# Row loads with the depth outermost, a limit on how far the maxima run ahead, and the first chunk's tail behind the last maximum

## The reference

```python
q, k, v = x @ Wq.T + bq, x @ Wk.T + bk, x @ Wv.T + bv          # 16 heads of depth 8
scores = einsum('bqhd,bkhd->bhqk', q, k) * attn_scale           # chunk-causal mask (64)
out = softmax(where(mask, -inf, scores)) @ v
x1 = layernorm(x + out @ Wo.T + bo)
sfc = sigmoid(x1 @ gate.T) + bias                               # 4 of 8 groups, then 6 of 32 experts
combine = weights of the chosen six, normalised, * 2.5
y = sum_e combine[:, e] * (silu(x1 @ g_e.T) * (x1 @ u_e.T)) @ d_e.T + shared(x1)
result = layernorm(x1 + y)
```

## Time and profile before

| | us |
|---|---|
| median of 3 runs | 496.4 (492.8 to 497.02) |
| the profiled execution | 494.91 |
| its span | 493.1 |

### The profile page before, as it was taken

One profiled execution on the slowest core, in us unless ns is written; L12 is line 12 of the kernel. 1 busy time (PEld: TensorE's weight loads), 2 busy tenths in 40 slices (PEclk: granted clock), 3 DMA queues, 4 the chain that ended last, 5 costly groups with the idle time before them and its releaser, 6 DMA issues.

```text
span 493.1 us, 7763 instructions
## 1 busy us (share of the span) xinstructions
PE 444.3 (90%) x2665; PEld 210.1 (43%) x2665; DVE 350.3 (71%) x848; ACT 223.1 (45%) x300; POOL 141.9 (29%) x244
## 2 busy tenths in 40 slices
PE   5429999999999999999799879899999999999992
PEld 2302232323333232433223323367676676666660
DVE  2619988888988888777987331286768869965863
ACT  4520016766857767677215369723242243223220
POOL 4061333756746362533213442400000000000000
PEclk9955558999999999998858869999999999999997
DMA  3434214420010101000000030033323322543330
GB/s 117 163 137 148 89 42 141 128 72 26 27 52 24 45 20 50 3 1 1 7 2 2 1 87 1 1 97 103 107 72 100 111 90 86 148 133 105 109 106 21
DMA packets 27031, 34.22 MB, mean 69 GB/s; under 512 B 5745, under 2 KB 16113, under 8 KB 26993
## 3 DMA queue, kind: packets, MB, share of 16 engines
q1 hardware_dynamic: 25862, 33.00, 21.7%
q10 hardware_dynamic: 1130, 0.74, 0.5%
HBM read 29.07 MB, written 4.46 MB: 68 GB/s over the span
## 4 chain that ended last, share of the span: by engine, by line
PE 73%; DVE 13%; DMA 4%; issue 3%; ACTq 3%; ACT 2%; POOL 2%; DVEq 0%; SPq 0%; POOLq 0%
PE ps L1338 13%; PE ps L1255 13%; PE ps L1380 11%; DVE mx L983 9%; PE ps L1353 6%; PE ps L1355 6%; PE ps L1354 6%; PE ps L1321 6%; PE ps L1251 6%; DMA rows_k<-scratch 2%; ACT probs L880 2%; ACTq L568 2%; PE ps L1268 1%; DMA wq<-in_wqT 1%; ACTq L603 1%
## 5 line engine op out<-in xcount | busy, mean ns | idle before, releaser
L983 DVE TENSOR_REDUCE mx<-ps 128x2 f32<-128x256 f32 (+3 forms) x384 | 191.0, 552 | 43.8 <-PE ps L1255 42.4
L880 ACT ACTIVATE probs<-ps 128x1024 f32<-128x1024 f32 (+2 forms) x160 | 142.8, 939 | 76.8 <-PE ps L1321 69.9
L1255 PE MATMUL ps<-rows_k,rows_q 48*128 48x128 bf16 (+3 forms) x576 | 117.6, 313 | 5.2 <-DVE mx L983 3.2
L1338 PE MATMUL ps<-probs,Vg 128*32 128x512 f32 (+3 forms) x768 | 86.8, 526 | 1.2 <-POOL probs L754 1.0
L923 ACT ACTIVATE rows_q<-ps 128x512 f32<-128x512 f32 x68 | 40.7, 599 | 97.3 <-PE ps L1355 94.7
L1255 PEld LDWEIGHTS ps<-rows_k,rows_q 48*128 48x128 bf16 x576 | 35.5, 97 | 91.6 <-DVE mx L983 65.9
L750 POOL TENSOR_SCALAR_AFFINE_SELECT probs<-probs 64x512 f32<-64x512 f32 x64 | 42.4, 662 | 110.4 <-ACT probs L880 108.9
L1353 PE MATMUL ps<-x1hi,w_hi 128*128 128x512 f32 x136 | 74.0, 544 | 0.0
L1321 PE MATMUL ps<-rows_q,rows_k 51*128 51x512 bf16 (+3 forms) x384 | 67.8, 347 | 4.0 <-ACT probs L880 3.9
L1380 PE MATMUL ps<-rows_k,w_down 128*128 128x512 f32 x136 | 69.5, 593 | 0.7 <-DVE rows_k L1199 0.7
L1194 DVE TENSOR_TENSOR rows_q<-ps,rows_q 128x512 f32<-128x512 f32 x64 | 44.1, 689 | 36.2 <-PE ps L1380 34.9
(11 more groups left out here) (105 smaller groups left out, 326.6 us busy)
## 6 DMA issues: line engine op xcount, KB each, us to landing
comb_rows<-weights SPq DMA_DIRECT2D x128, 128.0 KB, 3.0
scratch<-oT SPq DMA_DIRECT2D x8, 384.0 KB, 5.6
w_raw<-in_unitT SPq DMA_DIRECT2D x17, 128.0 KB, 5.7
rows_q<-scratch SPq DMA_DIRECT2D x16, 96.0 KB
rows_k<-scratch SPq DMA_DIRECT2D x14, 96.0 KB
w_down<-in_unitT SPq DMA_DIRECT2D x1, 1088.0 KB, 6.3
xT<-in_xT SPq DMA_DIRECT2D x4, 256.0 KB, 5.6
rows_q<-scratch SPq DMA_DIRECT2D x16, 64.0 KB
```

Source lines behind the costliest of these rows:

```text
L880: act.activation(dst, src, ACT.Exp).then_inc(exps_ready, 1)
L983: dve.tensor_reduce(to, src, AX.X, ALU.max).then_inc(max_read, 1)
L1255: mm = pe.matmul(dst[:, at * m:(at + 1) * m], rows_q[f:f + ROWS, s, p + qt * P:p + (qt + 1) * P], rows_k[f:f + ROWS, s, p + k0:p + k0 + m] ...
L1338: mm = pe.matmul(ps[STRIP * j:STRIP * (j + 1), VALUES * BANK:VALUES * BANK + m], Vg[:, g % 2, kt, j, :], probs[:, (NB * g + b) % SLOTS, j, ...
```

## The change

Four edits. The source of each row load has its depth dimension (8) outermost instead of its part dimension (3 or 2), so the rows land in another order, the same for q and k. The tail of chunk 0 starts behind the last maximum. The planner holds a maximum unit back while it is more than 1.6 groups ahead of the exponentials. The wait for the mask constants stands once ahead of the attention order instead of at the first unit.

```diff
@@ -132,7 +132,7 @@
 
 
 TOP_AFTER = 3
-TAIL_FROM = (NG - 2, 6)
+TAIL_FROM = (NG, 0)
 TOPS_BEFORE = [[t for t in TOPS if t[0] < g_] for g_ in range(NG)]
 MSEQ = max_steps()
 MAX_AT = {step: r for r, step in enumerate(step for step in MSEQ if step[0] in ON_BANK)}
@@ -163,6 +163,7 @@
     ev, vv = ([(g, n) for g in range(NG) for n in range(k)] for k in (NE, NB))
     hop, rows_latency, load = 240, 6000, 6000
     exp_slack, mask_slack = 300, 600
+    lead = 1.6
     t = 0.0
     clock = {"act": 0.0, "pool": 5000.0}
     dve = 0.0
@@ -238,6 +239,8 @@
     def ready_m():
         k = i["m"]
         kind, g, n = MSEQ[k]
+        if kind == "unit" and g + n / NM - i["e"] / NE > lead and i["e"] < len(ev):
+            return far
         out = 0
         if kind in ON_BANK and MAX_AT[kind, g, n] >= RING:
             out = read.get(RSEQ[MAX_AT[kind, g, n] - RING], far)
@@ -587,19 +590,20 @@
         def load_q(eng, g):
             b, r = g // GPB, slice((g % GPB) * STRIP, (g % GPB + 1) * STRIP)
             s = g % NS
-            part = scr[0, b, :, r, :].rearrange("h (d f p) t -> f h d (p t)", d=D, f=2)
+            part = scr[0, b, :, r, :].rearrange("h (d f p) t -> f d h (p t)", d=D, f=2)
+
             for f in range(2):
-                for at, n, src in ((0, 24, part[f]), (24, 16, part[f, 0:2]), (40, 8, part[f, 0])):
+                for at, n, src in ((0, 24, part[f]), (24, 16, part[f, :, 0:2]), (40, 8, part[f, :, 0])):
                     eng.dma_start(rows_q[ROW_HALF * f + at:ROW_HALF * f + at + n, s, :],
                                   src).then_inc(rows_loaded[s], 16)
 
         def load_k(eng, g):
             b, r = g // GPB, slice((g % GPB) * STRIP, (g % GPB + 1) * STRIP)
             s = g % NS
-            part = scr[1, b, :, r, :].rearrange("h (d f p) t -> f h d (p t)", d=D, f=2)
+            part = scr[1, b, :, r, :].rearrange("h (d f p) t -> f d h (p t)", d=D, f=2)
             for f in range(2):
-                for at, n, src in ((0, 24, part[f, 0:1].to_broadcast([3, D, PAIRS * T])),
-                                   (24, 16, part[f, 1:2].to_broadcast([2, D, PAIRS * T])), (40, 8, part[f, 2])):
+                for at, n, src in ((0, 24, part[f, :, 0:1].to_broadcast([D, 3, PAIRS * T])),
+                                   (24, 16, part[f, :, 1:2].to_broadcast([D, 2, PAIRS * T])), (40, 8, part[f, :, 2])):
                     eng.dma_start(rows_k[ROW_HALF * f + at:ROW_HALF * f + at + n, s, :],
                                   src).then_inc(rows_loaded[s], 16)
 
@@ -1224,6 +1228,8 @@
                     mm = pe.matmul(bank(VPROJ[n], P, t * P), xT[:, tt * P:(tt + 1) * P], wv[:, :], start=True, stop=True)
                 mm.then_inc(v_projected, 1)
 
+            pe.wait_ge(masks_loaded, 32)
+
             def max_step(kind, g, n):
 
                 r = MAX_AT[kind, g, n]
@@ -1242,8 +1248,6 @@
                 if kind != "unit":
                     tail_step(kind, g, n)
                     return
-                if r == 0:
-                    pe.wait_ge(masks_loaded, 32)
                 js, qt, k0, m, part = MAXU[g][n]
                 s, dst = g % NS, step_bank((kind, g, n), len(js) * m)
                 if part == 0:

```

## The result

The changed kernel takes 482.5 us (median of 4 runs, 481.63 to 483.17) against 496.6 us for the kernel before on the same chip (492.8 to 497.02). The ratio is 0.973, 95% interval 0.968 to 0.978. The forecast was 480 us, with a range of 472 to 489.

What follows compares the result with a forecast made beforehand. PE was taken to bound the steady part, with DVE near. Gains of 8.0 and 18.2 less costs of 3.3 and 7.5 made -15.4 on 494.91, so 479.5; the median forecast was 480 us, range 472 to 489.

Steps and rivals of the forecast that it cites:

- Term A: Row loads at the start: spread over more DMA engines, the first maximum comes near 26, a gain of 8.0 us.
- The full 8.0 passes: From first maximum to first exponentials and beyond: POOL's splits are off the path, so the whole 8.0 us gain carries on.
- Term B: Weave of chunk 0's tail, from 203 to the last transpose of maxima: 52.0 us instead of 70.2, a gain of 18.2.
- the density estimate of 53.4: Weave without the tail: 53.4 us if DVE keeps the density that it has in the steady part.
- the 54 that the prediction named as a sign of being wrong: Weave up to the last transpose of maxima: a stretch longer than 54 us would show the forecast wrong.
- Term C: From the last transpose of maxima to the first `up`: added chunk 0 and 1 steps cost 3.3 us.
- Term D: Start of the expert loop: first `down` about 11.4 us behind first `up` instead of 5.6, a cost of 7.5 us.
- behind it the hidden product of `i` = 0, for which up(2)'s second half waits: Expert loop start: DVE runs this 0.7 us product behind chunk 1's first route step, holding up(2) and so first `down`.
- U: Time of the first `up`; chunk 1's first route step on DVE was forecast to end 10.0 us behind it.
- That the loads don't spread: Rival for the row loads: they don't spread, or POOL's splits hold the exponentials; gain 0 to 3, 485 to 488; chance 0.10.
- That chunk 1's chain turns all it lacks into PE waits: Rival behind the maxima: chunk 1's chain lacks 9 us, all becoming PE waits; 489 us; chance 0.14.
- That the clock stays at half: Rival from last maximum to the loop's steady part: waits multiply, clock stays at half, +20 us, 500; chance 0.04.

Runs made afterwards that it cites:

- the three kernels with 12, 24 and 34 rows on the fullest one: Changed kernel (12, 482.5 us); changed kernel with the part dimension outermost again in its 16-partition row loads (24, 487.1 us); kernel before (34, 496.6 us).
- loads-only kernel: The kernel before with only the row-load edit of the change, all engine orders as before: 488.4 us, ratio 0.987.
- the kernel with the shared K load: Changed kernel with group 0's six K-load DMAs shared, four issued by ACT and the last two by SP: 480.3 us, ratio 0.967.
- The four kernels of the table above: Changed kernel (482.5 us); with chunk 1's route steps one loop step later (483.7); with the banked-step wait moved ahead of first `down` (484.9); with both (480.3).
- the version with the tail in the last group: Changed kernel with chunk 0's tail woven between the maxima of group 7 instead of behind the last maximum: 480.0 us, ratio 0.970.
- tail alone: Changed kernel with the row loads of before, all else as changed: 488.5 us, ratio 0.987.
- route step later: Changed kernel with chunk 1's route steps one step of the expert loop later: 483.7 us, ratio 0.968.
- banked wait later: Changed kernel with PE's wait for the last three banked steps' readers moved from ahead of up(2) to ahead of first `down`: 484.9 us, ratio 0.979.

## Why the prediction was right, point by point

**Term A, the row loads: the cause was right, the size was not.** That the loads fill more engines with the depth outermost is shown by the packet counts and by the three kernels with 12, 24 and 34 rows on the fullest one. POOL's waits for `w_raw` fell from 19.8 us in two places to 7.8 us in three, and the long queue is gone, though not wholly: the worst landing is 6.4 us, the best still 2.0. Term A took that best landing for the last K row. It was the step that failed: a small transfer's landing stood for that of six loads under way together, and no row showed the two to be alike. The rows land 4.0 us behind the issue (3.4 to 4.0 in seven executions), and the first maximum is at 27.64, not 26. The loads-only kernel (27.06) says the same.

**"The full 8.0 passes" failed as well.** The six stores of the first tops and the splits were not in the way, as argued (first exponential 72.31 before, 65.82 after: 6.5 us earlier, all that the first maximum had gained). Behind it 1.6 us went to a clock that stayed at half for longer, which the prediction had not looked at in that place. It need not have happened: the loads-only kernel has the same loads and a clock of 0.79 there, and loses nothing. In the kernel with the shared K load the clock rose early, and there the tops of group 3 come 8.5 us ahead of before.

**Term B, the weave: right.** The forecast was 52.0 us for the stretch and clock 1.0 throughout; the trace has 52.7 and 1.00. DVE's 45.92 busy in 52.73 is 0.87, the density of the steady part (48.13 of 54.90, 0.88), so the density estimate of 53.4 was the nearer of the two ways to count, and PE's 49.5 a bound from below. The pause of 9.99 us on ACT is gone. The longest one left in the attention, 5.83 us, holds the issue of the last maxima's six row DMAs, 4.56 us, and was there before too, ahead of 274.50 (5.84 us):

```profile
247.46 4.56 ACTq L571 DMA_DIRECT2D rows_q<-mh  x6
...
252.12 1.94 ACT L884 ACTIVATE probs<-ps 128x1024 f32<-128x1024 f32 x2 [5.83 <-issue]
```

The loads-only kernel, with 70.05 us in the same stretch, shows that the gain is the tail's alone. "Clock 1.0" was in part luck of the execution: four of the nine profiled kernels with this tail had 0.94 to 0.97 in the same stretch and took 54.1 to 55.4 us, above the 54 that the prediction named as a sign of being wrong.

**Term C: right in size.** 3.6 us for a forecast of 3.3, with the wait at comb that it named: 0.97 us for DVE's `work` at 283.99, for a forecast of 0.5 to 1. The router took from 276.92 to 283.84 on DVE, 6.9 us for an estimate of 6.6.

**Term D: right in size, wrong in what is waited for.** The first `down` came 11.8 us behind `up`, forecast 11.4, and the cost was 6.5 for 7.5. But the step "behind it the hidden product of `i` = 0, for which up(2)'s second half waits" names the second of two waits. The first is that for the last three banked steps ahead of the loop, which the prediction did not read out of the code: with chunk 1's logits among them, it ends with ACT's exponential behind a table load. The four kernels of the table above show both, and that removing either alone brings 0.3 us or nothing of the distance. The chain that the prediction did name ran as forecast up to the hidden product (U + 9.7, forecast U + 10.0), but PE then needed 1.5 us for the second half at the low clock, not 0.7. PE's wait at up(2) was 2.24 us, below the 3 that the prediction gave as a sign. Of the 1.7 us added for a low clock, 0.3 came behind the first `down`; the rest of D's 6.5 is the distance. ACT's timeline in the changed kernel has the rest as forecast, in order and in length:

```profile
299.69 0.59 ACT L908 CAST x1hi<-ps 128x512 fp32r<-128x512 f32 x1 [4.25 <-PE ps L1290]
300.29 1.28 ACT L927 ACT_TABLE_LOAD   x1
301.59 1.08 ACT L927 ACTIVATE rows_q<-ps 128x512 f32<-128x512 f32 x2
302.56 0.59 ACT L888 COPY oT<-ps 128x512 f32<-128x512 f32 x1
303.17 1.28 ACT L913 ACT_TABLE_LOAD   x1
304.46 0.28 ACT L913 ACTIVATE work<-ps 128x128 f32<-128x128 f32 x1
306.61 1.28 ACT L927 ACT_TABLE_LOAD   x1 [1.87 <-DVE rows_k L1206]
307.90 0.60 ACT L927 ACTIVATE rows_q<-ps 128x512 f32<-128x512 f32 x1
```

The first two table loads start 0.01 and 0.02 us behind the instruction before them, the third waits for DVE; each takes 1.28 us, and the next instruction starts 0.01 or 0.02 us behind it. No drain of 1.38 us, as the Trainium skill has it ("ScalarE: Activation LUTs", "What ACT_TABLE_LOAD costs"), shows here either. The prediction put 1.4 us on it for one switch; its own chain in D holds two, so with drains D would have been 2.8 us longer. The lower clock behind the waits came too: 0.88 over this stretch.

**The rivals.** That the loads don't spread is excluded by the first maximum and the packet counts. That chunk 1's chain turns all it lacks into PE waits did not come: PE waited 0.97 at comb, 0.60 at x1T and 2.24 at up(2), 3.8 us in place of 9. That the clock stays at half did not either: 0.89 from the last transpose to `up`.

**The sum.** -15.4 was forecast and -12.3 came in the profiled executions. Of the 3.1 us between them, A makes 3.1 (1.5 at the first maximum, 1.6 to the clock), B 0.7 and C 0.3, and D gave 1.0 back. The forecast of the median missed by 2.5 us. By its own sum it should have been 481.0 and not 480: the sum gives 479.5 for the profiled execution, and the median of before lay 1.5 above that.

## What to carry to other kernels

Look at the outermost dimension on the DRAM side of a load: 8 in place of 3 and 2 was worth 1.3% here. The sign in the profile was a small transfer that landed in 2 us at best and 10 at worst while half of the DMA engines idled, and the count of small packets shows how far a load spreads. A side chain woven into a stream whose reader is near its limit cost more than its own time here, because the streams that depend on it ran dry and the clock fell with them. Put it where that stream has ended, or where the others still have work in store, as in the version with the tail in the last group. Before pricing a moved step, list every wait that an in-order engine has at its new neighbours, not only the one that holds the data: here two waits, whose ends lay under 2 us apart with 1.5 us of matmuls between, hid each other, and removing one showed next to nothing.

## What the runs showed that was not expected

- The same work at the same place runs at a different clock in different executions: over 12 us from the first exponential the granted clock was 0.53 to 0.80 in thirteen kernels that hardly differ there, and a third of the time at half clock went into the end.
- Executions of one kernel fell into groups 5 to 9 us apart in three kernels (tail alone, route step later, banked wait later). Four profiled executions, two of them of an upper group, had a low clock at the same place of the weave, which makes 1 to 3 us of it. Traces of both groups of one kernel would be needed to say where the rest goes.
- Moving two of six K loads to another queue brought the last row 1.5 us forward in the mean of three executions, while the issue became 1.1 us shorter.
- The profile's count of small packets grew by 159 and 351 with loads spread over more engines, at the same data packets.
